# Attention of a two-block kernel: VectorE's part of the order placed behind TensorE's, two part buffers, merged narrow steps, and half of the output projection within the last quad

## The reference

```
q = (x @ Wq.T + bq).reshape(b, l, 32, 16).transpose(0, 2, 1, 3)     # k and v alike
scores = einsum('bhqd,bhkd->bhqk', q, k) / sqrt(16)
scores = where(causal, scores, -inf)
att = softmax(scores, axis=-1)
out = einsum('bhqk,bhkd->bhqd', att, v).transpose(0, 2, 1, 3).reshape(b, l, 512)
return out @ Wo.T + bo
```

## Time and profile before

| | us |
|---|---|
| median of the runs shown | 4374.48 |
| the profiled execution, its own time | 4376.63 |
| its span | 4374.9 |
| TensorE busy | 3951.7 (90%) |
| VectorE busy | 2711.7 (62%) |
| ScalarE, GpSimd busy | 1695.0, 1819.8 |
| mean granted TensorE clock | 0.903 |

### The profile page before, as it was taken

One profiled execution on the slowest core, in us unless ns is written; L12 is line 12 of the kernel. 1 busy time (PEld: TensorE's weight loads), 2 busy tenths in 40 slices (PEclk: granted clock), 3 DMA queues, 4 the chain that ended last, 5 costly groups with the idle time before them and its releaser, 6 DMA issues.

```text
span 4374.9 us, 61678 instructions
## 1 busy us (share of the span) xinstructions
PE 3951.7 (90%) x18308; PEld 2853.3 (65%) x18308; DVE 2711.7 (62%) x5034; ACT 1695.0 (39%) x3538; POOL 1819.8 (42%) x1951
## 2 busy tenths in 40 slices
PE   7899799779999999979778997997899999999797
PEld 5444477557777777757654444775577777777576
DVE  3557344567777777764435574445677777777644
ACT  1334411245555555542113344112455555555411
POOL 1111332345565665544311113323455556555543
PEclk8677899899999999989976778998999999999899
DMA  3221011011000110001132210110110001100011
GB/s 71 35 35 31 28 44 36 19 37 32 23 26 29 34 31 26 24 15 44 38 75 35 35 31 28 44 36 19 37 32 25 24 29 34 31 27 23 15 45 40
DMA packets 80974, 145.13 MB, mean 33 GB/s; under 512 B 16152, under 2 KB 18056, under 8 KB 80784
## 3 DMA queue, kind: packets, MB, share of 16 engines
q1 hardware_dynamic: 80784, 142.84, 12.4%
HBM read 112.64 MB, written 4.19 MB: 27 GB/s over the span
## 4 chain that ended last, share of the span: by engine, by line
PE 71%; issue 11%; DVE 7%; ACT 4%; POOL 2%; DVEq 2%; POOLq 1%; SPq 1%; DMA 1%; ACTq 0%
PE banks L485 15%; PE banks L486 14%; PE banks L487 14%; PE banks L826 4%; PE banks L665 4%; PE banks L646 3%; PE banks L622 3%; PE banks L819 2%; PE banks L839 2%; DVE conv L1338 2%; PE banks L529 2%; DVEq L1341 1%; PE banks L761 1%; PE banks L762 1%; POOL X L1503 1%
## 5 line engine op out<-in xcount | busy, mean ns | idle before, releaser
L1338 DVE SCALAR_TENSOR_TENSOR conv<-banks,cpar,conv 128x509 f32<-128x509 f32 (+2 forms) x576 | 428.2, 744 | 115.9 <-ACT conv L999 101.5
L1166 DVE TENSOR_TENSOR Y<-banks,Y 128x512 f32<-128x512 f32 x400 | 275.6, 691 | 233.5 <-PE banks L487 233.2
L942 ACT ACTIVATE probs<-banks 128x1024 f32<-128x1024 f32 (+3 forms) x384 | 298.1, 809 | 310.4 <-PE banks L646 309.5
L622 PE MATMUL banks<-stack_k,stack_q 48*128 48x512 f32 (+3 forms) x768 | 335.9, 510 | 58.8 <-DVEq L1212 19.6
L1573 POOL TENSOR_SCALAR_AFFINE_SELECT probs<-probs 128x256 f32<-128x256 f32 x256 | 104.2, 408 | 663.2 <-ACT probs L942 662.9
L1637 POOL TENSOR_TENSOR state<-state,gt 128x512 f32<-128x512 f32 x112 | 133.5, 1192 | 499.5 <-PE banks L819 499.5
L1484 POOL TENSOR_SCALAR f_hi<-f_raw 128x512 fp32r<-128x512 f32 x150 | 93.8, 625 | 581.4 <-PE banks L487 472.7
L485 PE MATMUL banks<-xhi,f_hi 128*128 128x512 f32 x800 | 328.5, 411 | 3.5 <-DVE xlo L1137 3.5
L485 PE MATMUL banks<-xhi,wx_hi 128*128 128x512 f32 x768 | 312.6, 407 | 15.9 <-DVE conv L1338 15.9
L486 PE MATMUL banks<-xhi,f_lo 128*128 128x512 f32 x800 | 319.9, 400 | 0.0
L487 PE MATMUL banks<-xlo,f_hi 128*128 128x512 f32 x800 | 319.5, 399 | 0.0
(11 more groups left out here) (203 smaller groups left out, 10353.5 us busy)
## 6 DMA issues: line engine op xcount, KB each, us to landing
m_raw<-in_w_mamba SPq DMA_DIRECT2D x224, 256.0 KB, 2.6
f_raw<-in_w_ffn SPq DMA_DIRECT2D x50, 768.0 KB, 4.6
stack_q<-part_hi SPq DMA_DIRECT2D x128, 64.0 KB, 2.4
stack_k<-part_hi SPq DMA_DIRECT2D x128, 64.0 KB, 2.5
X<-in_x SPq DMA_DIRECT2D x4, 1024.0 KB, 6.6
wqk_raw<-in_w_attn SPq DMA_DIRECT2D x8, 512.0 KB, 3.5
stack_q<-part_lo SPq DMA_DIRECT2D x64, 64.0 KB, 2.4
stack_k<-part_lo SPq DMA_DIRECT2D x64, 64.0 KB, 2.5
```

Of the source, the lines that this page charges most:

```text
L622: r = pe.matmul(dst[:, 0:cols], stack_q[buf][base:base + ROWS, h, i * P:(i + 1) * P], stack_k[buf][base:base + ROWS, h, s * HALF:s * HALF ...
L942: act.activation(probs[n % 2][:, 2 * p:2 * p + 2, 0:w], banks[:, 2 * p:2 * p + 2, 0:w], ACT.Exp, scale=1.0 / HD ** 0.5).then_inc(exp_done[ ...
L1166: dve.tensor_tensor(Y[:, i, :], bank[6 + i % 2], Y[:, i, :], ALU.add).then_inc(f["dn_used"], 1)
L1338: r = dve.scalar_tensor_tensor(out=rest, in0=src[:, 0:HALF - lag], scalar=cpar[:, o:o + 1], in1=rest, op0=ALU.mult, op1=ALU.add)
```

## The change

1. **Order.** TensorE's and VectorE's (and ScalarE's) halves of a use become entries of their own: proj / proj_hi / proj_lo, values_in / values_out, maxima / maxima_out, turn / turn_out, the second one placed later. A projection is issued in two halves of six matmuls, after two successive steps; its proj_lo comes two steps after the second half. Of f = 1 two uses stand among the first pieces and two in quad 0; f = 2 lies in quads 0 and 1, f = 3 in quads 2 and 3 (PROJ_STEPS). Two value tiles stand before the first piece instead of five.
2. **Banks.** Before the first score the ring has seven banks (4, 5, 7, 0, 1, 2, 3), then the same three as before. A use takes the bank whose last use is freed earliest in ORDER instead of the next in rotation, and waits for that one's release.
3. **Part buffers.** A second pair of part buffers lies in X, which is free after the normalisation. X is loaded again (`load_x`) once the last stack has landed, and `add_normed` waits for that. Stacks have a semaphore per parity and head, so the first pieces of a head wait for its six DMAs only. SP's queue is reordered: load_qk(1) before stack(0), and from t = 2 on stack(t + 1) directly before put_maxima(t).
4. **Steps.** The last two of each half (256 and 128 wide) are one step of 384 columns: 10 steps in a quad instead of 12, with the same matmuls and two Exps fewer per merged pair of steps.
5. **Output projection.** Token tiles 0 to 3 (EARLY) are turned and projected in quad 7 after steps 5 to 9; the weights are split by GpSimd in quad 6, one k at a time. PROJ has tiles 4 to 7.

```diff
-                part_hi = sb("part_hi", [P, 2, L], F32R, stack=s2)
+                part_hi = [sb("part_hi", [P, 2, L], F32R, stack=s2)[:]]
+                part_lo = [sb("part_lo", [P, 2, L], F32R, stack=s2)[:]]
+                for part, h in ((part_hi, 0), (part_lo, 1)):
+                    own = X[:, h * CPH:(h + 1) * CPH, :].rearrange("p (w u) d -> p w (u d)", w=2)
+                    part.append(own.bitcast(F32R))
...
-        STEPS = [(s, j) for s in range(2) for j in range(CPH * (s + 1))]
+        STEPS = [(s, (j,) if j < CPH * (s + 1) - 2 else (j, j + 1)) for s in range(2) for j in range(CPH * (s + 1) - 1)]
...
+        EARLY = 4
+        MAIN_BANKS, FIRST_BANKS = (4, 5, 7), (4, 5, 7, 0, 1, 2, 3)
+
+        PROJ_STEPS = {}
+        for f, use, t, n in ((1, 2, 0, 0), (1, 3, 0, 2), (2, 0, 0, 6), (2, 1, 1, 0), (2, 2, 1, 3), (2, 3, 1, 6),
+                             (3, 0, 2, 2), (3, 1, 2, 6), (3, 2, 3, 0), (3, 3, 3, 4)):
+            PROJ_STEPS[t, n], PROJ_STEPS[t, n + 1] = (f, use, 0), (f, use, 1)
...
+            for i in range(2):
                 yield "values_in", i
+                yield "values_out", i
             for n in range(NP):
+                if n % 6 == 3 and n < 36:
+                    yield "values_in", 2 + n // 6
+                if n % 6 == 2 and 2 < n < 42:
+                    yield "values_out", 1 + n // 6
+                if n in (36, 40, 43, 46):
+                    yield "proj", 1, int(n > 40), int(n in (40, 46))
+                if n in (40, 46):
+                    yield "proj_hi", 1, int(n > 40)
+                if n == 45:
+                    yield "proj_lo", 1, 0
+                yield from some(1)
             yield "maxima", 0
+            yield from some(2)
+            yield "maxima_out", 0
...
             for t in range(NQ):
                 for n in range(NS):
                     for q in range(QUAD):
                         yield "score", t, n, q
                         if n == NS - 2 and q == 1 and t + 1 < NQ:
                             yield "maxima", t + 1
+                        turning = n == NS - 2 and q < 2 and t + 1 < NQ
+                        more = n < NS - 2 and q == 0 or n in (0, 4) and q == 2
+                        yield from some(0 if turning else 2 if more else 1)
+                        if n == NS - 2 and q == 2 and t + 1 < NQ:
+                            yield "maxima_out", t + 1
+                        if q == 1 and n == 3 and t > 0:
+                            yield "turn_out", t - 1, 1
+                        if q == 1 and n == (7 if t + 1 < NQ else 5):
+                            yield "turn_out", t, 0
+                        if q == 2 and (t, n - 2) in PROJ_STEPS and PROJ_STEPS[t, n - 2][2]:
+                            yield "proj_lo", *PROJ_STEPS[t, n - 2][:2]
                     if n > 0:
                         yield "values", t, n - 1
-                    if n == 1 and t > 0:
+                    if n == 2 and t > 0:
                         yield "turn", t - 1, 1
-                    if n == 7:
+                    if n == (6 if t + 1 < NQ else 4):
                         yield "turn", t, 0
+                    if t + 1 == NQ and n >= NS - 1 - EARLY:
+                        i = n - (NS - 1 - EARLY)
+                        if i < EARLY:
+                            yield "at", i
+                            yield "at_hi", i
+                            yield "at_lo", i
+                        if i > 0:
+                            yield "out", i - 1
+                            yield "out_add", i - 1
+                    if (t, n) in PROJ_STEPS:
+                        yield "proj", *PROJ_STEPS[t, n]
+                        if PROJ_STEPS[t, n][2]:
+                            yield "proj_hi", *PROJ_STEPS[t, n][:2]
...
+        def ring_banks():
+            last, bank_of, before = {}, {}, {}
+            for use in RING_USES:
+                main = ORDER.index(use) >= ORDER.index(("score", 0, 0, 0))
+                allowed = MAIN_BANKS if main else FIRST_BANKS
+                k = min(allowed, key=lambda i: (last[i][2] if i in last else -1))
+                bank_of[use[:3]], before[use[:3]] = k, last.get(k)
+                last[k] = release(use)
...
+                load_qk(1)
                 stack(0)
                 stack(1)
-                load_qk(1)
+                put_maxima(0)
+                load_qk(2)
                 held(sp, v_used, b + 1)
                 ones_in(1)
-                put_maxima(0)
-                load_qk(2)
                 stack(2)
-                stack(3)
                 put_maxima(1)
-                put_maxima(2)
                 load_qk(3)
...
+                for t in range(2, NQ):
+                    if t + 1 < NQ:
+                        stack(t + 1)
+                    else:
+                        held(sp, pv_done, b * (NQ * NS) + (NQ - 2) * NS)
+                        sp.dma_start(wo_raw[:], w_attn[3 * KT:4 * KT].rearrange("n p c -> p n c")).then_inc(wo_in, 16)
+                        sp.dma_start(bo_sb[:], bo).then_inc(wo_in, 16)
                     put_maxima(t)
+                for par in range(2):
+                    for h in range(QUAD):
+                        held(sp, stacked[par][h], (b + 1) * (NQ // 2 * STACKED))
+                load_x(b)
```

More of the change, by code:

```diff
@@ new lines, in build, with some, project @@
+        EARLY = 4
+        AHEAD = 6
+        MAIN_BANKS, FIRST_BANKS = (4, 5, 7), (4, 5, 7, 0, 1, 2, 3)
[3 more added lines that the diff above has]
+            PROJ_STEPS[t, n], PROJ_STEPS[t, n + 1] = (f, use, 0), (f, use, 1)
+        def attention_order():
+            pieces = [(t, n) for t in range(NQ) for n in range(NP)]
+            def some(count):
+                for _ in range(count):
+                    if pieces:
+                        yield "piece", *pieces.pop(0)
+            def project(f, use):
+                yield "proj", f, use, 0
+                yield "proj", f, use, 1
+                yield "proj_hi", f, use
+                yield "proj_lo", f, use
@@ L281, in attention_order @@
             for use in range(4):
-                yield "proj", 0, use
-            for i in range(5):
+                yield from project(0, use)
+            for i in range(2):
                 yield "values_in", i
+                yield "values_out", i
             for n in range(NP):
[L286 to L290, removed]
@@ new lines, in build, with release @@
+        RING_ENDS = [o[:3] for o in ORDER if o[0] in ("piece", "values_in", "maxima", "turn") or o[0] == "proj" and o[3]]
+        RING = len(RING_ENDS)
+        FREED = {"piece": "piece", "values_in": "values_out", "turn": "turn_out"}
+        FREES = [o for o in ORDER if o[0] in FREED.values()]
+        FREE = len(FREES)
+        def release(use):
+            kind, *arg = use
+            if kind == "proj":
+                return "part_lo_ready", 4 * arg[0] + arg[1] + 1, ORDER.index(("proj_lo", *arg[:2]))
+            if kind == "maxima":
+                return "mt_ready", arg[0] + 1, ORDER.index(("maxima_out", *arg))
+            if kind == "at":
+                return "at_free", arg[0] + 1, ORDER.index(("at_lo", *arg))
+            if kind == "out":
+                return "o_free", arg[0] + 1, ORDER.index(("out_add", *arg))
+            end = (FREED[kind], *arg)
+            return "ring_free", FREES.index(end) + 1, ORDER.index(end)
@@ L669, in _ @@
-                        r.then_inc(pv_done, 1)
+                        for j, lo, at, w in blocks(n):
+                            for h in range(QUAD):
+                                r = pe.matmul(bank[6][32 * h:32 * h + VW, lo:HALF], V[:, j, QUAD * t + h, :],
+                                              probs[n % 2][:, h, at:at + w], start=j == 0,
+                                              stop=j == CPH * (s + 1) - 1, skip_group_check=True,
+                                              tile_position=(0, 32 * h))
@@ L1201, in _ @@
                 held(dve, mask_built, b + 1)
-                ring = 0
                 for what, *arg in ORDER:
-                    if what == "proj":
+                    if what == "proj_lo":
                         f, use = arg
```

309 lines of the change are left out of this document (162 added, 147 removed).

## The result

The changed kernel takes 4466.73 us (median of 4 runs, 4464.80 to 4469.36) against 4378.17 of the kernel before beside it: ratio 1.0208, 95% interval 1.0182 to 1.0234. I had forecast 4244. The profiled execution took 4466.15 us, its span is 4464.4.

The account below looks back on a forecast made before the run. TensorE carries 71% of the chain, alternating with VectorE in early pieces and bounding plain quads, half the time at 1.2 GHz. Terms -28 - 25 + 2 - 10 - 4 = -65 us a batch, -130 together: 4244, forecast range 4170 to 4310.

Parts of the forecast that it names:

- Part 1: First pieces: new order, seven banks and per-head semaphores bring the first score at 103 instead of 131.3, -28 us a batch.
- Part 2: Quads 0 to 3, then with ten projections: stops go and the clock rises, 206.0 to 181 us, -25 a batch.
- I give 2 us a quad for it: Quads 0 to 3: allowance for pieces having two banks in 25 of 40 steps while a projection holds one.
- Rival C: Quads 0 to 3: a projection's held bank puts pieces in lockstep, +60 us; +18 a batch overall, 4413; chance 0.05.
- If the clock rises from about 0.69 to 0.8: Quads 0 to 3: assumed clock gain, 60% of the time at full speed, plain quad 34 us, projection 3.7.
- 0.4 x 39: Plain quad's half-clock share: 40% of the time at 39 us a quad, within the 34 us estimate.
- half clock throughout, 4 x 39.5 + 51 = 209: Quads 0 to 3: slow bound if the clock stays at half, +3 us a batch.
- Part 3: Quads 4 to 6: merged steps leave fewer holes, 35.5 us a quad, 116.7 to 106.5, -10 a batch.
- Part 4: Quad 7 and output projection: early tiles fill 4 of 6.4 us of holes, -4 a batch, bounds +3 and -6.
- Waits added: Quads 0 to 3: GpSimd's weight split +1 us and put_maxima behind SP's stack issue +1, +2 a batch.
- Rival B: Clock stays at 0.65 to 0.7 although gaps close: -15 up to -25 us a batch, about 4337; chance 0.20.
- A: Clock goes full as the stops go, VectorE bounds at 28 to 29 us a quad: -119 a batch, 4138; chance 0.15.

Follow-up runs that it names:

- short hold: Changed kernel with both halves of a projection issued together and proj_lo in the next step, against the kernel before: 4330.97 us, ratio 0.9887.
- short hold and turns as before: Changed kernel, steps still merged, projections issued whole with proj_lo in the next step, turns placed as in the kernel before: 4319.74 us, ratio 0.9877.
- the last variant: Changed kernel unmerged, projections whole with proj_lo next step, turns as before (4290.38 us), plus weight splits moved where no mask precedes them: 4279.52 us, ratio 0.9803.

## Why the prediction was wrong

**Part 1 was right**, near its upper bound: -36 for -28. The first score came at 95.1 with a clock of 0.90 where I had taken 0.85, VectorE's stops at part_lo and V are gone. The clock alone doesn't give it: busy x clock is 39.49 x 0.90 = 36 us and not my 43. No run takes the semaphores, the seven banks or the new order away, so their shares aren't shown.

**Part 2 failed**, +54 for -25, outside its own bounds (+3 to -54), and +61 in the second batch. The 54 us are 22.9 of idle time and 31.5 of longer busy time. Three terms of it:
- "I give 2 us a quad for it", for two banks instead of three. The short hold shows 58 us in four quads, some 15 a quad. Rival C named the mechanism and its place, at +60 a batch; that its size is near is luck, for it priced stalls alone, and 44 of the 58 us are longer busy time at a lower clock. I dismissed it because 1.34 / 2 = 0.67 us a piece on two banks is under the 0.83 that a piece gets. The trace shows what that average hid. Where a turn falls into the hold there is one bank and 1.5 us a piece; and pieces don't come evenly, so that even with two banks free they waited 17.9 us. TensorE runs its list in order, so scores and values stand behind the waiting piece.
- "If the clock rises from about 0.69 to 0.8". It went to 0.67. I had tied the clock to the stops that went, and not to those that the hold would bring.
- "0.4 x 39", the time of a quad at half clock. I took it from the mean of quads that had been at half clock for half to two thirds of their time (mean clock 0.66 to 0.74). Quads nearly all at half clock take 47 to 49 us in the changed kernel. The bound "half clock throughout, 4 x 39.5 + 51 = 209" was no bound; with 48 it would have been 4 x 48 + 51 = 243, and even that leaves out the stalls. TensorE busy 10.00 of 10 us says nothing of how much of a quad is done in them; its 48 of a quad's 205 matmuls would have given some 43 us, as an estimate.

**Part 3 failed**, +28 for -10 (+16 in the second batch), bounds 0 to -24. The cause is the clock: 0.54 for 0.66 to 0.81 at the same work. I had counted merging as "nothing directly" and fewer holes as a gain. Merging in the new ring is what it goes with: unmerged, with the turns still late, quads 4 to 6 take 118.8. Taking the late turns back leaves four of six plain quads at 0.54. In the old ring the merged quads took 36 to 41 us in the one execution profiled. What of the new ring matters is untested: the choice of banks, the second part buffers and SP's order were in every variant but that one.

**Part 4**: the gain in it was real (8 us a batch), the sign of the sum wrong, again by the clock at which quad 7 starts.

**Waits added**: the wait for the maxima's DMA in quads 0 to 3 is 2.9 us in the first batch and 3.6 in the second, against 0.7 before; the split cost 2.6 and 2.5, against 3.5 before. Together some 1 to 2 us more, for the +2 forecast. These were sized rightly.

Rival B had the clock at 0.65 to 0.7 and took 4337 from it, because it used the same 39 us and nothing for stalls of the hold. The stretch that A and B both cite at 1.00, 29.2 to 60.4 us, reads a little too well: its matmuls at 31 us still come 0.43 us apart, as at half clock. My chances gave 0.05 to slower. The prediction's own signs read correctly afterwards: quads 1 and 3 outside 42 to 52 us (68.4, 62.1), a clock under 0.72 (0.66 over 100 to 380 us, which I had given to B), and pieces waiting for maxima more than 30 us a batch, 32.1 in the list above.

**Still open.** What decides whether the clock rises in a plain quad. With short hold and turns as before, quad 5 is the same instructions in either batch, and the starts of its steps 0 to 6 are alike to 0.02 us; in step 6 the clock rises in the first batch and not in the second:

```profile
330.30:371.40 41.10, 38.35 (x207) 16.99 (x203) 28.24 (x89) 18.69 (x20) 6.31 (x16) 0.71 0.21 36
2484.10:2532.00 47.90, 46.48 (x207) 20.20 (x203) 28.83 (x89) 18.76 (x20) 6.31 (x16) 0.54 0.18 30
```

Counted over quads 4 to 6 of both batches, the clock is 0.60 or more in 23 of 24 with unmerged steps, and in 21 of 48 with merged ones in the new ring. Many of these repeat the other batch to 0.1 us, so fewer are independent. The runs show that, and not why.

## What to carry to other kernels

Decoupling two engines by answering later costs the resource that is held meanwhile: before a consumer is moved back, count for every step how many banks of the ring are left, and don't divide by the average. A change of order can cost more through the TensorE clock than through the waits: 14 us of idle time came with 44 us of clock here. It need not: the last variant lost 8 us of idle time at an unchanged 0.81. To bound a stage, take its time at each of the two clock levels from stretches that were wholly at one level, never from a mean of both.

## What the runs showed of the hardware that I had not expected

- The same some 205 matmuls of quad 4 or 5 take 36 us at a mean clock of 0.88, 39 to 42 at about 0.75 and 46 to 49 at about 0.54, while VectorE's work in it stays at 28 to 29 us. TensorE is busy 89% of the time in the first and 95% or more in the last.
- The low level can last through long stretches in which TensorE hardly pauses. One of them, in quad 4 of the changed kernel:

```profile
370.00:380.00 10.00, 9.82 (x47) 4.10 (x45) 7.07 (x24) 4.28 (x5) 0.00 (x0) 0.50 0.00 1
```
